# Second attention of a two-layer gated cross-attention kernel: the product with the values turned round, with a new order of the steps

## The reference

```
q, k, v = layernorm(x) @ Wq + bq, ctx @ Wk + bk, ctx @ Wv + bv      # by heads of 8
scores  = (q . k + q . rel_key_table[ids]) / sqrt(8)                # ids = clip(i - j, -128, 128) + 128
attn    = softmax(scores)                                           # over the 77 context tokens
out     = attn . v + attn . rel_value_table[ids]
x       = x + tanh(g_xattn[1]) * (out @ Wo + bo)
```

## Time and profile before

| | |
|---|---|
| median of three runs | 2222.26 us |
| the profiled execution's own time | 2223.91 us |
| its span in the profile | 2222.1 us |
| PE, DVE, ACT, POOL busy, share of the span | 94%, 86%, 70%, 72% |
| granted TensorE clock, mean | 0.972 of full speed |
| second attention, about | 1207 to 1823 us |

### The profile page before, as it was taken

One profiled execution on the slowest core, in us unless ns is written; L12 is line 12 of the kernel. 1 busy time (PEld: TensorE's weight loads), 2 busy tenths in 40 slices (PEclk: granted clock), 3 DMA queues, 4 the chain that ended last, 5 costly groups with the idle time before them and its releaser, 6 DMA issues. The chain is left out here.

```text
span 2222.1 us, 82115 instructions
## 1 busy us (share of the span) xinstructions
PE 2087.2 (94%) x28058; PEld 1635.8 (74%) x28060; DVE 1916.7 (86%) x4322; ACT 1554.5 (70%) x3452; POOL 1597.9 (72%) x1521
## 2 busy tenths in 40 slices
PE   3999999977999999999995999999999976999999
PEld 1788888854666666666663999999999973666666
DVE  5899999987888888898895888888888878888888
ACT  3788888865556565555553777777777756888887
POOL 1577777643666666666665999999999943888887
PEclk9899999987999999999997999999999988999999
DMA  5000000004332332222321455555555530000000
GB/s 155 11 6 6 6 6 6 7 1 97 90 89 76 85 85 79 86 83 77 90 66 36 77 78 78 78 78 78 78 78 78 80 74 8 10 14 14 9 14 14
DMA packets 476442, 121.39 MB, mean 55 GB/s; under 512 B 431879, under 2 KB 446855, under 8 KB 475604
## 3 DMA queue, kind: packets, MB, share of 16 engines
q1 hardware_dynamic: 343988, 86.86, 18.5%
q10 hardware_dynamic: 132384, 33.63, 6.6%
HBM read 106.51 MB, written 13.89 MB: 54 GB/s over the span
## 5 line engine op out<-in xcount | busy, mean ns | idle before, releaser
L1219 POOL TENSOR_TENSOR f_low<-f_hidden,f_high 128x512 f16<-128x512 f32 x336 | 442.3, 1321 | 217.3 <-ACT f_high L1151 215.4
L1177 DVE TENSOR_TENSOR f_hidden<-f_hidden,f_share 128x512 f32<-128x512 f32 x336 | 374.1, 1114 | 0.0
L1366 POOL TENSOR_TENSOR f_low<-f_hidden,f_high 128x512 f16<-128x512 f32 x256 | 296.4, 1159 | 74.4 <-ACT f_high L1309 74.2
L1157 ACT ACTIVATE f_act_out<-f_gate 128x512 f32<-128x512 f32 x336 | 200.4, 596 | 192.6 <-PE f_gate L1121 192.6
L1200 DVE SCALAR_TENSOR_TENSOR f_hidden<-f_up,f_act_out 128x512 f32<-128x512 f32 x336 | 229.8, 684 | 82.7 <-PE f_up L1121 50.6
L1742 POOL TENSOR_TENSOR a_q_head_high<-a_q_t_high,a_head_mask 128x2048 f16<-128x2048 f16 x64 | 233.0, 3640 | 55.3 <-PE a_score L1544 47.2
L1151 ACT ACTIVATE f_high<-f_hidden 128x512 f16<-128x512 f32 x336 | 210.5, 627 | 72.9 <-DVE f_hidden L1177 71.6
L1131 PE MATMUL f_y<-w_high,f_high 128*128 128x128 f16 x1344 | 242.4, 219 | 2.2 <-POOL f_low L1219 2.2
L1131 PE MATMUL f_y<-w_low,f_high 128*128 128x128 f16 x1344 | 242.4, 219 | 0.0
L1131 PE MATMUL f_y<-w_high,f_low 128*128 128x128 f16 x1344 | 242.4, 219 | 0.0
L1742 POOL TENSOR_TENSOR a_q_head_low<-a_q_t_low,a_head_mask 128x2048 f16<-128x2048 f16 x64 | 232.8, 3637 | 0.0
(11 more groups left out here) (269 smaller groups left out, 8521.2 us busy)
## 6 DMA issues: line engine op xcount, KB each, us to landing
f_share<-expert_shares SPq DMA_DIRECT2D x128, 256.0 KB, 3.2
a_q_pos<-queries ACTq DMA_DIRECT2D x64, 512.0 KB, 3.9
f_share<-expert_shares SPq DMA_DIRECT2D x128, 128.0 KB, 3.1
relative_values<-a_rel_all SPq DMA_DIRECT2D x512, 8.0 KB, 1.7
x_all<-in_x SPq DMA_DIRECT2D x4, 1024.0 KB, 8.1
f_share<-expert_shares SPq DMA_DIRECT2D x128, 32.0 KB, 1.8
queries<-a_q_parts SPq DMA_DIRECT2D x64, 64.0 KB, 4.0
a_rel<-relative_values SPq DMA_DIRECT2D x64, 64.0 KB, 3.2
```

The costliest lines, as they stand in the source:

```text
L1157: nc.scalar.activation(act_out[m % RING][:, :], gate_ps[m % BANKS][:, :], ACT.Silu, scale=1.0 / WSCALE).then_inc(act_ready, 1)
L1177: nc.vector.tensor_tensor(hidden[r][:, :], hidden[r][:, :], share[k][:, :, :].rearrange("p t q -> p (t q)"), ALU.mult).then_inc(scaled, 1)
L1219: nc.gpsimd.tensor_tensor(low[r][:, :], hidden[r][:, :], high[r][:, :], ALU.subtract).then_inc(low_ready, 1)
L1366: nc.gpsimd.tensor_tensor(low[k][:, :], hidden[k][:, :], high[k][:, :], ALU.subtract).then_inc(low_ready, 1)
```

## The change

It is all in `relative_attention`.

1. The rows of a turned tile change from (query, head) to (head, query): the transpose multiplies by a permuted identity, `by_head_ident`. The tile of probabilities itself is as before. The DMAs of `write_relative` pick their partitions accordingly, eight apart.
2. `mix`: the values become the weights, padded with zeros to 32 columns per head (`VW`), and the probabilities of a head are the moving operand, 128 columns in 16 runs of 8. Four heads write to four groups of 32 partitions of a new bank `rows_ps`, which are four column tiles of the array. The output has values in partitions and queries in columns.
3. So it has to be turned back: `copy_rows` (ACT) copies the bank to `mixed_rows`, `mix_turn` (PE) transposes its four quarters into `mix_ps`.
4. `fin_ps` and `mix_ps` become one bank. `fin_turn` waits in addition for the sums of the sequence after it, `mix_turn` for the residual of the sequence before the one before it.
5. `add_bias` on POOL goes; `fin_project` gets a fourth product that adds the bias, from rows split into high and low before the loop.
6. The order of the slots is written anew on PE, ACT, POOL and DVE. `read_queries` stands first on ACT, `add_relative` a slot earlier on POOL, the first two `row_max` and the first `subtract_max` of a sequence at the end of DVE's slot before.

```diff
-        value = [sb(f"value{p}", [KC, NH, 2 * (HD + 1)], F16) for p in range(2)]
+        value = [sb(f"value{p}", [KC, NH, VW], F16) for p in range(2)]
+        mixed_rows = sb("mixed_rows", [P, QUARTERS, P])
+        by_head_ident = sb("by_head_ident", [P, NH, QC])
-        prep_ps, rel_ps, mix_ps, fin_ps = ps("prep"), ps("rel"), ps("mix"), ps("fin")
+        prep_ps, rel_ps, rows_ps, mix_ps = ps("prep"), ps("rel"), ps("rows"), ps("mix")
+        fin_ps = mix_ps
...
-                            sp.dma_start(r_written[p][c], rel_all[p][NH * c:NH * (c + 1), :, HD * c:HD * (c + 1)]
+                            sp.dma_start(r_written[p][c], rel_all[p][c:P:QC, :, HD * c:HD * (c + 1)]
...
                             mm = nc.tensor.transpose(trans_ps[u % 2][0:KC, P * j:P * (j + 1)], prob[u][:, j, :],
-                                                     ident[:, :])
+                                                     by_head_ident[:, :, :].rearrange("r h c -> r (h c)"))
...
+                def mix(n, p):
+                    if inside(n, 0, B):
+                        pe.wait_ge(prob_low, 4 * n + 4)
+                        pe.wait_ge(proj_low, n + 3)
+                        wait(pe, rows_copied, n)
+                        by_head = [t[:, :, :].rearrange("k g (h c) -> k g h c", h=NH) for t in prob_t[p]]
+                        for u in range(QUARTERS):
+                            own = [rows_ps[VW * j:VW * (j + 1), P * u:P * (u + 1)] for j in range(4)]
+                            for j in range(4):
+                                nc.tensor.matmul(own[j], value[p][:, 4 * u + j, :], by_head[0][:, :, 4 * u + j, :],
+                                                 start=True, stop=False, skip_group_check=True)
+                            for j in range(4):
+                                mm = nc.tensor.matmul(own[j][0:HD + 1, :], value[p][:, 4 * u + j, 0:HD + 1],
+                                                      by_head[1][:, :, 4 * u + j, :], start=False, stop=True,
+                                                      skip_group_check=True)
+                        mm.then_inc(mix_ready, 1)
+
+                def mix_turn(n):
+                    if inside(n, 0, B):
+                        pe.wait_ge(rows_copied, n + 1)
+                        wait(pe, x_ready, n - 1)
+                        for u in range(QUARTERS):
+                            mm = nc.tensor.transpose(mix_ps[:, P * u:P * (u + 1)], mixed_rows[:, u, :], ident[:, :])
+                        mm.then_inc(rows_turned, 1)
...
                 def fin_turn(n, p):
                     if inside(n, 0, B):
                         pe.wait_ge(mixed_ready, n + 1)
+                        pe.wait_ge(summed, min(n + 2, B) if isinstance(n, int) else n + 2)
+                        pe.wait_ge(rden_ready, min(n + 2, B) if isinstance(n, int) else n + 2)
...
+                        mm = nc.tensor.matmul(fin_ps[:, 0:D], sel[:, :], out_rows[:, :], start=False, stop=True)
...
+                def copy_rows(n):
+                    if inside(n, 0, B):
+                        act.wait_ge(mix_ready, n + 1)
+                        wait(act, rows_turned, n)
+                        nc.scalar.activation(mixed_rows[:, :, :].rearrange("r u q -> r (u q)"), rows_ps[:, :],
+                                             ACT.Copy).then_inc(rows_copied, 1)
```

More of the change, by code:

```diff
@@ L27 @@
 KT = KC + P - QC
+QUARTERS, VW = 4, P // 4
 QB = 2 * HD
@@ L1566, in relative @@
                         mm.then_inc(rel_ready, 1)
-                def mix(n, p, half):
+                def mix(n, p):
                     if inside(n, 0, B):
[L1570 to L1583, removed]
+                        pe.wait_ge(prob_low, 4 * n + 4)
[12 more added lines that the diff above has]
+                        mm.then_inc(mix_ready, 1)
@@ L1601, in slot @@
                     scores(n, p, 0)
+                    scores(n, p, 1)
                     turn(n - 1, 2)
+                    fin_project(n - 4, p)
+                    relative(n - 1, o, 0)
+                    turn(n - 1, 3)
                     project(n, p)
-                    relative(n - 1, o, 0)
-                    scores(n, p, 1)
-                    turn(n - 1, 3)
+                    mix_turn(n - 2)
                     relative(n - 1, o, 1)
-                    fin_project(n - 4, p)
                     scores(n, p, 2)
+                    scores(n, p, 3)
+                    fin_turn(n - 3, o)
+                    relative(n - 1, o, 2)
                     turn(n, 0)
-                    relative(n - 1, o, 2)
-                    mix(n - 1, o, 0)
+                    turn(n, 1)
+                    mix(n - 1, o)
                     prep_turn(n + 3, o)
-                    scores(n, p, 3)
-                    turn(n, 1)
                     relative(n - 1, o, 3)
-                    mix(n - 1, o, 1)
-                    fin_turn(n - 3, o)
                 pe.wait_ge(weights_ready, 2)
@@ L1625, in _ @@
                 pe.wait_ge(table_ready, 1)
-                pe.wait_ge(bias_split, 5)
+                pe.wait_ge(bias_split, 6)
                 slots(pe, FIRST, LO, HI, LAST, slot)
@@ L1729, in _ @@
                 for p in range(2):
-                    for k in range(2):
-                        own = (HD + 1) * k + HD
-                        nc.gpsimd.memset(value[p][:, :, own:own + 1], 1.0 - k)
+                    nc.gpsimd.memset(value[p][:, :, HD:HD + 1], 1.0)
+                    nc.gpsimd.memset(value[p][:, :, 2 * HD + 1:VW], 0.0)
                     last = nc.gpsimd.memset(q_pos[p][:, :, :], 0.0)
@@ L1760, in divide @@
                                                 ALU.mult).then_inc(mixed_ready, 1)
-                def add_bias(n):
-                    if inside(n, 0, B):
-                        pool.wait_ge(xn_ready, n + 1)
-                        nc.gpsimd.tensor_tensor(x_all[:, n, :], x_all[:, n, :], b_o[:, :], ALU.add).then_inc(x_biased, 1)
                 def slot(n, p):
                     o = 1 - p
+                    divide(n - 3, o)
                     mask_queries(n + 1, o)
-                    add_relative(n - 3, o)
-                    add_bias(n)
-                    divide(n - 3, o)
+                    add_relative(n - 2, p)
                 slots(pool, -1, LO, HI, B + 3, slot)
@@ L1799, in _ @@
                 nc.vector.tensor_tensor(b_o[:, :], b_o[:, :], fin_ps[:, 0:D], ALU.add).then_inc(weights_ready, 1)
+                dve.wait_ge(weights_ready, 3)
+                nc.vector.tensor_copy(out_rows[:, :], b_o[:, :]).then_inc(out_bias, 1)
+                dve.wait_ge(out_bias, 1)
+                nc.vector.tensor_tensor(b_o[:, :], b_o[:, :], out_rows[:, :], ALU.subtract).then_inc(out_bias, 1)
+                dve.wait_ge(out_bias, 2)
+                nc.vector.tensor_scalar(b_o[:, :], b_o[:, :], ident[:, 1:2], None, ALU.mult).then_inc(out_bias, 1)
+                dve.wait_ge(out_bias, 3)
+                nc.vector.scalar_tensor_tensor(out=out_rows[:, :], in0=out_rows[:, :], scalar=ident[:, 0:1], in1=b_o[:, :],
+                                               op0=ALU.mult, op1=ALU.add).then_inc(out_bias, 1)
                 def low_xn(n, p):
@@ L1881, in slot @@
                     o = 1 - p
-                    row_max(n, 0)
-                    low_mixed(n - 4, p)
-                    subtract_max(n, 0)
+                    subtract_max(n, 1)
                     low_prob(n - 1, o, 2)
+                    sum_parts(n - 2, p)
                     inverse_sum(n - 2, p)
-                    row_max(n, 1)
-                    sum_parts(n - 2, p)
-                    subtract_max(n, 1)
                     low_prob(n - 1, o, 3)
-                    residual(n - 4)
+                    row_max(n, 2)
                     low_parts(n, p)
-                    row_max(n, 2)
-                    statistics(n - 4)
-                    subtract_max(n, 2)
-                    low_prob(n, p, 0)
-                    row_max(n, 3)
-                    low_xn(n + 3, o)
-                    subtract_max(n, 3)
-                    low_prob(n, p, 1)
+                    subtract_max(n, 2)
+                    row_max(n, 3)
+                    subtract_max(n, 3)
+                    low_prob(n, p, 0)
+                    low_mixed(n - 3, o)
+                    low_prob(n, p, 1)
+                    low_xn(n + 3, o)
+                    row_max(n + 1, 0)
+                    row_max(n + 1, 1)
+                    residual(n - 3)
+                    subtract_max(n + 1, 0)
+                    statistics(n - 4)
                 slots(dve, FIRST, LO, HI, LAST, slot)
```

45 lines of the change are left out of this document (26 added, 19 removed).

## The result

| | before | after |
|---|---|---|
| median of five runs each | 2222.70 us (2221.87 to 2223.28) | 2210.74 us (2208.10 to 2213.86) |
| ratio, 95% interval | | 0.9945 (0.9933 to 0.9957) |
| a slot of the second attention, mean of 30 | 9.24 us | 8.81 us |

The change makes the kernel faster, but by 12 us where 41 were forecast; 2210.74 lies inside the range and far from 2181. A repetition gave 0.9949 (0.9932 to 0.9966) and 8.85 us.

The account below looks back on a forecast made before the run. TensorE's queue was taken as the bound: slot 9.19 - 1.98 (old mix) + 0.475 + 0.06 + 0.79 = 8.53 us. 63 slots save 41.6 us, setup adds 0.5: median 2181 us, range 2167 to 2214.

Parts of the forecast that it names:

- s = 20 ns: New mix on TensorE: assumed time per product in four column tiles, between 14 and 26 ns; 32 products plus 0.15 us.
- The doubled stream: Mix's moving operand in runs of 8 f16: each run might cost double, at most +0.4 us a slot; taken as nothing.
- Rival 3: Mix: the four tiles run one after another, 57 ns a product, mix 1.97 us, slot 9.71, 2255 us; chance 0.08.
- Rival 2: Mix: loads in column tiles are not hidden, eight rounds 1.31 us, slot 9.20, 2222 us, no change; chance 0.07.
- PE's slot: Second attention on TensorE: 9.19 us a sequence falls to 8.53, namely 7.74 plus 0.79 for the new mix.
- The setup: Before the loop: four small DVE operations for out_rows, 1.3 us together, mostly covered by idleness; +0.5 us, 0 to +1.3.
- they land before a read that a slot of 8.5 us still leaves time for: SP's eight relative writes, now from partitions eight apart: they land in time for their read, so no cost.
- POOL's cycle gets no longer by it: POOL: add_relative moves one slot earlier, in front of the next mask, at no cost; POOL busy 8.39 us a slot.
- So I cost the new waits at nothing: PE's order in the slot: waits for DVE's residual and sums have about 1 us slack or more; cost nothing.
- keep count and size, 3.76 us of issue: SP: the eight relative writes, from partitions eight apart, still take 3.76 us to issue.
- rival 1: Queries' round trip holds PE, deciding from a 5 us landing; at 5.3, slot 8.85 and 2201 us; chance 0.14.
- when `turn 0` wants ACT, 6.31: ACT behind read_queries and copy_rows: exp 0 done by about 5.3 us in the slot, turn 0 needs it at 6.31.

Follow-up runs that it names:

- e7: e3 with the mix's eight products of one column tile issued before the next tile's, instead of four tiles in turn: 2219.47 us, ratio 0.9981 to the kernel before.
- e3: Changed kernel with queries' write ahead of read_relative on SP and POOL's mask split in halves around add_relative, a sequence later: 2184.62 us, ratio 0.9814 to the kernel before.
- e1: Changed kernel with the write of the queries issued ahead of read_relative on SP: 2219.87 us, ratio 0.9978 to the kernel before.
- e4: Changed kernel with the eight relative writes reading neighbouring partitions again (values reach wrong places): 2198.70 us, ratio 0.9881 to the kernel before.
- e5: Changed kernel with the plain identity in the turn, so the mix's moving operand takes every sixteenth f16, writes from neighbouring partitions: 2258.55 us, ratio 1.0157 to the kernel before.

## Why the prediction was right in its terms and wrong in its sum

- **The mix.** Forecast 0.79 us with s = 20 ns; it is 0.56 with 14 ns, the lower end, and 0.09 more in front of it. For the tiles that is 0.20 (0.09 entering, 0.11 leaving) instead of 0.15. The doubled stream was rightly left out. Rival 3 (tiles in turn, 1.97 us) fell; e7 shows what half of it would cost. Rival 2 fell with it: with 14 ns a product there is no room for a load that isn't hidden. By the Trainium skill, TensorE: Matmul & The Clock Gate, Part 3 (The mechanism), a load overlaps products in flight only where the row group differs; all tiles here share theirs, and the trace disagrees. The same section also lets a load run ahead when it goes to the background weight buffer; whether that is what happens here, no run shows.
- **PE's slot.** 8.53 forecast, 8.475 in e3, where nothing else holds it, and 8.36 of that is work. The slot before was read once, 9.19; slots of 9.27 and 9.20 take turns there, 9.24 as a mean.
- **The clock** stayed at 1.00. **The setup** took its four DVE operations, 1207.58 to 1208.76, in the place forecast.
- **The step that failed: the round trips of SP and POOL were put at nothing, by "they land before a read that a slot of 8.5 us still leaves time for" and "POOL's cycle gets no longer by it".** I laid out PE's and DVE's slot in full and judged SP and POOL by sentences. ("So I cost the new waits at nothing" was said of `mix_turn` and `fin_turn`, and there it held.) Four things were missing. First, "keep count and size, 3.76 us of issue": the issue became 5.11 us, and from the first write to the landing it went from 5.00 us (1504.06 in the earlier trace rows, the read at 1509.06) to 6.80. Second, "POOL's cycle gets no longer by it" looked at the sum of POOL's work and not at the order: with `add_relative` a slot earlier, its read's landing comes in front of 8.15 us of POOL's work that the next scores need. Third, the queries' write stands on SP behind that read, so it was issued some 1.8 us after its data were there. The DMA itself was quicker than taken, 3.0 us and not 4.0, so the landing came late by 0.9: 4.9 us from data to landing, close to the 5 us from which rival 1 decides. Fourth, the sum asked only when `turn 0` wants ACT, 6.31; the first to wait is `relative 1` at 4.07, for the `copy_relative 0` behind `copy_rows`. All this is harmless at a slot of 9.2; at 8.5 both chains, 8.84 and 8.75 us, are longer.
- **Rival 1** had the place (a landing of the queries holds ACT, slot 8.85, 2201 us). That the slot's size agrees is in part luck: the cause was a late issue and not a slow landing, and it lacked the second chain, so its cure alone, e1, gives nothing. The rise in the time of the writes alone is not the cause either (e4).
- **From slot to total.** 63 x 0.43 = 27 us would be expected from the slot; 12 came, 13.7 between the two profiled executions. The first `statistics` came 58.9 us after the operation on `a_w_out_low` in the setup (L1797, after the change L1819) instead of 52.5; the slots of the filling show PE waiting:

```profile
1247.51 0.66 PE L1596 MATMUL a_mix<-ident,a_mixed_rows 128*128 128x128 f32 x4 [1.85 <-ACT a_mixed_rows L1722]
...
1268.76 1.06 PE L1596 MATMUL a_mix<-ident,a_mixed_rows 128*128 128x128 f32 x4 [2.40 <-ACT a_mixed_rows L1722]
```

  So 6.4 us more went by before it, of which the forecast had 0.5. The loss goes on for a few slots: the sixth `statistics` comes at 1314.96 instead of 1307.48, 7.5 us later, where five slots less 0.43 each would have put it 2.2 us sooner. Of the 13.4 us missing 9.6 are thus in the filling, a term that the forecast did not have, and the rest comes later, in the loop and in the draining. e3 shows the same: 63 x (9.24 - 8.475) = 48 us by the slot and 41 in the total. There the low s and the low 9.19 cancel against the missing term, so that e3's 41 us equal the forecast by luck.

What stays open: why an issue from partitions eight apart takes longer, and why the landing grew. For the second the rows suggest that transfers now meet: after the change the 512 KB read of the queries is issued 1.5 us after the first of the writes (1507.79 against 1506.31), before it 4.1 us (1508.18 against 1504.06). The other runs speak against this as the main cause. In e1 and e7 that read comes 4.6 and 5.0 us after the first write, and the stretch is still 6.56 and 6.48 us; in e5, with neighbouring partitions and 4.7 us, it is 5.86, against 5.00 before the change (all means from 1400 to 1600 us). The two rows of the kernel before that the earlier trace rows lack, SP's read and ACT's read of the queries:

```profile
1509.06 0.34 SPq L1492 DMA_DIRECT2D a_rel<-relative_values  x1
...
1508.18 0.37 ACTq L1639 DMA_DIRECT2D a_q_pos<-queries  x1
```

## What to carry to other kernels

When a change shortens the engine that sets the pace, follow every chain that goes out through a DMA and comes back, over as many slots as it spans, with queue, issue and landing, and divide by those slots: what was slack at the old pace is the new bound. Where the expected gain is missing and two engines wait for transfers, undo the waits in pairs before calling either innocent, for two chains of one length hide each other. And where a transpose is made anyway, a permuted identity in it can turn a scattered operand into runs of 16 bytes.

## What the runs showed of the hardware that I had not expected

- Four column tiles take f16 products of 128 columns at 14 ns each (0.056 us a round of four), loads of 32 and 9 columns hidden; leaving them costs 0.11 us and entering 0.09.
- Every sixteenth f16 as the moving operand costs 0.23 us a round, 4.1 times the time in runs of 8.
- Tiles that follow one another in the program still overlap by about half: 1.27 us for 32 products, against 0.56 abreast and 32 x 0.057 = 1.82 in turn.
- Eight DMAs from partitions eight apart took 5.11 us to issue, 0.64 each, from neighbouring ones 3.76, 0.47 each; the shorter issue (e4) shortened the time to the landing by 0.30 us only.
